# Kv heads in pairs between the row maxima and the output rows of a gated cross-attention block

## The reference

```python
# x and ctx (8, 256, 512) fp32; H = 32 heads of D = 16, HK = 8 kv heads, G = 4 heads to one, T = 256
q = heads(concat([ctx, layernorm(x)]) @ Wq)          # (B, 32, 256, 16)
k, v = heads(layernorm(x) @ Wk), heads(layernorm(x) @ Wv)
ssm_k, ssm_v = heads(ctx @ Wsk), heads(ctx @ Wsv)
scores = einsum('bhqd,bhkd->bhqk', q, concat([ssm_k, k])) / 4 + alibi   # 0 <= q - k < 64, else -inf
o = einsum('bhqk,bhkd->bhqd', softmax(scores), concat([ssm_v, v]))
x = x + tanh(g_xattn) * (o @ Wo)
x = x + tanh(g_ffn) * ffn(layernorm(x))              # router over 128 experts, top 4, a shared part
```

## Time and profile before

| | |
|---|---|
| time before, median of 3 runs | 914.48 us (913.05 to 917.12) |
| time of the profiled execution | 912.41 us |
| its span | 910.5 us |
| TensorE busy (matmul) | 883.1 us, 97% |
| weight loads | 764.3 us, 84% |
| VectorE, ScalarE, GpSimd busy | 568.0, 400.9, 515.8 us |
| mean granted TensorE clock | 0.991 |

### The profile page before, as it was taken

How to read it: one execution, slowest core, us unless ns; L and a number is a source line. 1 busy time by engine, 2 the same in 40 slices (tenths; PEclk the granted TensorE clock), 3 DMA queues, 4 the chain that set the end, 5 groups by cost and what they waited for, 6 DMA issues and landing times.

```text
span 910.5 us, 17708 instructions
## 1 busy us (share of the span) xinstructions
PE 883.1 (97%) x6694; PEld 764.3 (84%) x6694; DVE 568.0 (62%) x1107; ACT 400.9 (44%) x838; POOL 515.8 (57%) x562
## 2 busy tenths in 40 slices
PE   7989999999999999799999999999999999999998
PEld 7878999999999998587888876788888888888886
DVE  6666676767677766672235666565655656556657
ACT  6544545455545554555024243344444444444431
POOL 6561533434343430434188985455887888878731
PEclk9989999999999999999999999999999999999999
DMA  7678476767667565991101144512012120221036
GB/s 239 148 194 211 123 202 152 207 165 204 177 159 221 145 171 139 236 306 65 46 1 47 47 146 146 197 40 77 24 70 70 32 85 23 70 70 27 21 121 248
DMA packets 79358, 115.44 MB, mean 127 GB/s; under 512 B 6561, under 2 KB 49314, under 8 KB 78242
## 3 DMA queue, kind: packets, MB, share of 16 engines
q1 hardware_dynamic: 77000, 113.28, 44.1%
q10 hardware_dynamic: 2274, 1.03, 0.5%
HBM read 75.95 MB, written 36.24 MB: 123 GB/s over the span
## 4 chain that ended last, share of the span: by engine, by line
PE 88%; DMA 3%; SPq 2%; DVE 2%; issue 2%; ACT 2%; POOL 1%; POOLq 0%; DVEq 0%; ACTq 0%
PE ps_scores L2031 19%; PE ps_proj L1701 12%; PE ps_scoresT L2031 10%; PE ps_scores L1690 6%; PE ps_scoresT L1829 6%; PE ps_o L1843 6%; PE ps_scores L1808 6%; PE ps_proj L1690 5%; PE ps_scoresT L1690 5%; PE ps_proj L2031 5%; PE ps_proj L1757 4%; DMA q_stack<-max_rows 1%; SPq L552 1%; DMA w_stage<-in_L_xattn_Wv 1%; PE ps_o_max L1739 1%
## 5 line engine op out<-in xcount | busy, mean ns | idle before, releaser
L1023 ACT ACTIVATE probsT<-ps_scoresT 128x512 f32<-128x512 f32 (+1 forms) x256 | 137.4, 543 | 143.7 <-PE ps_scoresT L1829 143.4
L1347 DVE TENSOR_REDUCE neg_max<-ps_scores 128x2 f32<-128x384 f32 (+1 forms) x256 | 131.9, 517 | 91.9 <-PE ps_scores L1808 88.0
L1233 ACT ACTIVATE part_sums<-ps_scores 128x512 f32<-128x512 f32 x96 | 57.5, 599 | 134.8 <-PE ps_scores L2031 130.4
L1829 PE MATMUL ps_scoresT<-q_stack,k_stack 116*128 116x256 f32 x448 | 104.4, 304 | 10.5 <-ACT probsT L1023 5.8
L1808 PE MATMUL ps_scores<-k_stack,q_stack 114*128 114x192 f32 (+1 forms) x512 | 99.9, 278 | 2.5 <-DVE neg_max L1347 1.2
L1808 PEld LDWEIGHTS ps_scores<-k_stack,q_stack 114*128 114x128 f32 x512 | 82.0, 192 | 13.3 <-DVE neg_max L1347 2.9
L895 POOL TENSOR_TENSOR w_expert_lo<-w_sums,w_expert_hi 128x256 fp32r<-128x256 f32 x64 | 63.8, 1008 | 45.3 <-ACT w_expert_hi L1156 45.3
L907 POOL TENSOR_TENSOR big<-big,basis 128x512 f32<-128x512 f32 x56 | 77.5, 1401 | 15.5 <-DVE basis L1640 15.5
L760 POOL TENSOR_TENSOR oT_lo<-oT_raw,oT_hi 128x256 fp32r<-128x256 f32 x32 | 23.6, 737 | 105.8 <-ACT oT_hi L1034 105.8
L1829 PEld LDWEIGHTS ps_scoresT<-q_stack,k_stack 116*128 116x128 f32 x448 | 71.8, 195 | 12.8 <-issue 6.0
L754 POOL TENSOR_TENSOR o_normal<-o_blocks,inv_sums 128x128 f32<-128x128 f32 x64 | 25.8, 403 | 96.6 <-DVE inv_sums L1367 96.6
(11 more groups left out here) (286 smaller groups left out, 2540.3 us busy)
## 6 DMA issues: line engine op xcount, KB each, us to landing
k_stack<-k_kept SPq DMA_DIRECT2D x64, 192.0 KB, 5.8
q_stack<-q_kept SPq DMA_DIRECT2D x28, 384.0 KB, 5.5
big<-coeff_rows SPq DMA_DIRECT2D x8, 1024.0 KB, 4.8
q_kept<-qT_hi SPq DMA_DIRECT2D x12, 512.0 KB
xn_rows<-in_x SPq DMA_DIRECT2D x8, 512.0 KB, 5.9
k_kept<-kT_hi SPq DMA_DIRECT2D x16, 256.0 KB
x_rows<-in_x SPq DMA_DIRECT2D x8, 512.0 KB, 4.4
x_kept<-x_rows SPq DMA_DIRECT2D x16, 256.0 KB, 5.0
```

Of the source, the lines that this page charges most:

```text
L1023: act.activation(PT[:, g % 2, 2 * j:2 * j + blocks].rearrange("p h f r w -> p (h f r w)"), ST[:, n % 2, 0:blocks].rearrange("p h n -> p (h ...
L1233: act.activation(TP[:, u % 2, j, :], src[:, u % 2, :], ACT.Copy).then_inc(taken, 1)
L1347: dve.tensor_reduce(NM[:, g % 2, 2 * i:2 * i + 2], SA[:, n % 2, :, 0:keys], AX.X, ALU.max, negate=True).then_inc(max_done, 1)
L1829: ins = pe.matmul(ST[:, n % 2, v, :], KS[0:ROWS, g, j + v, 1 - v].rearrange("p w s -> p (w s)"), QS[0:ROWS, g, j + v].rearrange("p f r w - ...
```

## The change

Two neighbouring groups (a **pair**) are taken together from `max_halves` to `o_turn`. `max_halves`, `turn_max`, `max_out` and `stack_max` work on 16 columns of maxima and come once in 8 slots, at 8p + 8, 8p + 9, 8p + 9 and 8p + 10. `times_v` multiplies both groups one behind the other at slot 8p + 26, into the two halves of `ps_o`. `o_turn` turns the whole bank (128x512), `scale_outputs` scales both. The turned maxima move to the free half of the second bank of `ps_scoresT` (a group's last unit needs one half only), so that every odd unit of `scores_turned` waits for `nm_out` as well. `LAG` goes from 14 to 18 and all offsets behind it by 3 or 4 slots; the projections are laid into other slots, since the slots of `times_v` are now twice as long and half as many. `stack_q` reads one group at a time (192 KB), right behind `stack_k` of the same group, both 10 slots ahead of the group's first `scores` (before: keys 14 slots ahead, queries 10 or 14). Each engine's count of instructions: 64 `turn_max`, `max_out`, `stack_max`, `o_turn`, `scale_outputs` become 32; 28 DMAs of `stack_q` become 56.

```diff
-LAG = 14
-NM_TURN, PV, O_TURN, O_BACK, O_HIGH = 6, LAG + 5, LAG + 6, LAG + 8, LAG + 9
+LAG = 18
+PAIR = 2 * NB
+MAX_HALVES, NM_TURN, STACK_MAX = PAIR, PAIR + 1, PAIR + 2
+PV, O_TURN, O_BACK, O_HIGH = LAG + PAIR, LAG + PAIR + 1, LAG + PAIR + 3, LAG + PAIR + 4
 LOAD_ROWS, STATS = -64, (-51, -50)
-CTX_HIGH, CTX_LOW = (-44, -43), (-43, -42)
+CTX_HIGH, CTX_LOW = (-42, -41), (-41, -40)
-Q_PROJ = ((-31, -30, -28), (-27, -26, -24), (-23, -22, -20), (-19, -18, -16))
+Q_PROJ = ((-29, -28, -27), (-26, -25, -24), (-21, -20, -18), (-17, -16, -15))
...
-STACK_K = tuple(4 * g + LAG + 4 - UNITS for g in range(HK))
-STACK_Q = tuple(8 * p + LAG + 8 - UNITS for p in range(PAIRED))
+STACKED = tuple(NB * g + LAG + NB - UNITS for g in range(HK))
...
-def group_due(n, offset):
+def pair_due(n, offset):
...
-    g, rest = divmod(n - offset, NB)
-    return g if rest == 0 and 0 <= g < GROUPS else None
+    p, rest = divmod(n - offset, PAIR)
+    return p if rest == 0 and 0 <= p < GROUPS // 2 else None
+
+
+def max_turns(n):
+
+
+    return max(0, -(-(n - NM_TURN) // PAIR))
...
-ROUTER_AT = {0: 0, 4: 1, 12: 2, 30: 3}
-SHARED_AT = {15: 0, 17: 1, 20: 2, 23: 3, 25: 4, 28: 5}
+ROUTER_AT = {0: 0, 4: 1, 12: 2, 34: 3}
+SHARED_AT = {19: 0, 21: 1, 24: 2, 27: 3, 29: 4, 32: 5}
...
-    PO, PM = POB[:, 0, :], POB[0:4 * NB, 1, 0:P]
+    PM = ST[0:8 * NB, 1, 1, 0:P]
...
-        def stack_q(b, p):
-            gs = slice(2 * p, 2 * p + 2)
+        def stack_q(b, g):
             sp.wait_ge(q_kept, 16 * PARTS * b)
-            sp.wait_ge(st_mm, (b - 1) * UNITS + 2 * NB * (p + 1))
-            sp.dma_start(QS[DATA:FINE, gs].rearrange("p g i f r w -> p g (i f r w)").bitcast(F32),
-                         q_kept_d[b % 2, gs].rearrange("g j d n -> (j d) g n")).then_inc(q_in[p], 16)
+            sp.wait_ge(st_mm, (b - 1) * UNITS + NB * (g + 1))
+            sp.dma_start(QS[DATA:FINE, g].rearrange("p i f r w -> p (i f r w)").bitcast(F32),
+                         q_kept_d[b % 2, g].rearrange("j d n -> (j d) n")).then_inc(q_in[g], 16)
...
-        def turn_max(n):
-            pe.wait_ge(nm_lo, n + 1)
-            if n >= 1:
-                pe.wait_ge(nm_out, n)
-            if n > LEAD - 1:
-                pe.wait_ge(o_turned, n - LEAD + 1)
-            pe.transpose(PM, NMH[:, n % 2].rearrange("p h c -> p (h c)").bitcast(F32), ident[:]).then_inc(nm_t, 1)
+        def turn_max(p):
...
+            unit = PAIR * p + NM_TURN - LAG
+            pe.wait_ge(nm_lo, p + 1)
+            if unit >= 2:
+                pe.wait_ge(exp_done, unit - 1)
+            pe.transpose(PM, NMH[:, p % 2].rearrange("p h c -> p (h c)").bitcast(F32), ident[:]).then_inc(nm_t, 1)
...
+            if n % 2:
+                pe.wait_ge(nm_out, min(max_turns(n + LAG), GROUPS // 2))
...
-        def times_v(n):
-            b, g = divmod(n, HK)
+        def times_v(p):
+            b = p // (HK // 2)
             pe.wait_ge(turn_done, passed("turn_v", b, 0))
-            pe.wait_ge(exp_done, NB * (n + 1))
-            if n >= 1:
-                pe.wait_ge(o_turned, n)
-            pe.wait_ge(nm_out, min(n + LEAD, GROUPS))
-            for j in range(NB):
-                cols_j = min(2 * W, T - j * W)
-                for r in range(G):
-                    ins = pe.matmul(PO[32 * r:32 * r + 2 * D, j * W:j * W + cols_j], VA[:, j, g, :],
...
+            if p >= 1:
+                pe.wait_ge(o_turned, p)
+            for n in (2 * p, 2 * p + 1):
+                pe.wait_ge(exp_done, NB * (n + 1))
+                for j in range(NB):
+                    cols_j = min(2 * W, T - j * W)
+                    for r in range(G):
...
+                ins.then_inc(pv_mm, 1)
```

More of the change, by code:

```diff
@@ L105, in due @@
     return b if rest == 0 and first <= b < B else None
-def group_due(n, offset):
-    g, rest = divmod(n - offset, NB)
-    return g if rest == 0 and 0 <= g < GROUPS else None
+def pair_due(n, offset):
[3 more added lines that the diff above has]
+    return max(0, -(-(n - NM_TURN) // PAIR))
 def split_due(n):
-    found = [p for p in range(GROUPS // 2) if n == O_HIGH + NB * (2 * p + 1) + (NB if p == 0 else 0)]
+    found = [p for p in range(GROUPS // 2) if n == O_HIGH + PAIR * p + (2 if p == 0 else 0)]
     return found[0] if found else None
@@ L133, in x_turn_slot @@
 def x_turn_slot(b, t):
-    return (69, 72)[t] if b < B - 1 else (58, 59)[t]
+    return (73, 77)[t] if b < B - 1 else (62, 63)[t]
 def batch_at(n, slot, first=0):
@@ L301, in build @@
     k_kept, q_kept, pad_kept = sem("k_kept"), sem("q_kept"), sem("pad_kept")
-    stack_in, max_in = ([sem(f"{n}_in{g}") for g in range(HK)] for n in ("stack", "max"))
-    q_in = [sem(f"q_in{p}") for p in range(PAIRED)]
+    stack_in, q_in = ([sem(f"{n}_in{g}") for g in range(HK)] for n in ("stack", "q"))
+    max_in = [sem(f"max_in{p}") for p in range(HK // 2)]
     s_mm, max_done, nm_hi, nm_lo, nm_t, nm_out = (
@@ L599, in _ @@
             for g in range(HK):
-                b = due(n, STACK_K[g], 1)
+                b = due(n, STACKED[g], 1)
                 if b is not None:
                     stack_k(b, g)
-            for p in range(PAIRED):
-                b = due(n, STACK_Q[p], 1)
-                if b is not None:
-                    stack_q(b, p)
+                    stack_q(b, g)
             b = due(n, LOAD_ROWS, 2)
@@ L813, in _ @@
                 x1_normalise(b, 0)
-            m = group_due(n, O_TURN)
-            if m is not None:
-                scale_outputs(m)
+            p = pair_due(n, O_TURN)
+            if p is not None:
+                scale_outputs(p)
             b = batch_at(n, lambda b: x1_roots_slot(b) + (1 if b < B - 1 else 0))
@@ L1111, in _ @@
                 exponentials(n - LAG)
-            m = group_due(n, NM_TURN)
-            if m is not None:
-                max_out(m)
-            m = group_due(n, NM_TURN + 1)
-            if m is not None:
-                stack_max(m)
+            p = pair_due(n, NM_TURN)
+            if p is not None:
+                max_out(p)
+            p = pair_due(n, STACK_MAX)
+            if p is not None:
+                stack_max(p)
             if n == SPLIT_WO:
@@ L1435, in _ @@
         for n in range(SLOTS):
-            m = group_due(n, NM_TURN - 2)
-            if m is not None:
-                max_halves(m)
+            p = pair_due(n, MAX_HALVES)
+            if p is not None:
+                max_halves(p)
             if n < END:
                 maxima(n)
-            m = group_due(n, O_TURN)
-            if m is not None:
-                o_turn(m)
-            m = group_due(n, O_BACK)
-            if m is not None and m % 2:
-                o_back_turn(m // 2)
+            p = pair_due(n, O_TURN)
+            if p is not None:
+                o_turn(p)
+            p = pair_due(n, O_BACK)
+            if p is not None:
+                o_back_turn(p)
             for t in range(TB):
@@ L1801, in scores @@
                 if b >= 1:
-                    pe.wait_ge(q_in[g // 2], 16 * b)
+                    pe.wait_ge(q_in[g], 16 * b)
             if n >= 2:
@@ L1887, in gate_up @@
                 pe.wait_ge(exp_done, END)
+                pe.wait_ge(nm_out, GROUPS // 2)
             if q == FIRST_TILES + 1:
@@ L1918, in _ @@
                 scores(n)
+            p = pair_due(n, PV)
+            if p is not None:
+                times_v(p)
+            p = pair_due(n, NM_TURN)
+            if p is not None:
+                turn_max(p)
             if LAG <= n < END + LAG:
                 scores_turned(n - LAG)
-            m = group_due(n, NM_TURN)
-            if m is not None:
-                turn_max(m)
-            m = group_due(n, PV)
-            if m is not None:
-                times_v(m)
             for t in range(TB):
@@ L1968, in turn_logits @@
                 pe.wait_ge(turn_done, len(TURNS))
-                pe.wait_ge(o_turned, GROUPS)
-                pe.wait_ge(nm_out, GROUPS)
+                pe.wait_ge(o_turned, GROUPS // 2)
             for j in range(4):
```

83 lines of the change are left out of this document (41 added, 42 removed).

## The result

The paired kernel takes 923.54 us in the median (918.34 to 924.71), the kernel before, on the same chip, 914.6 us (913.05 to 917.12): a ratio of 1.0086, with a 95% interval of 1.0048 to 1.0124. It is slower by about 0.9%, where 908.6 was forecast with a range that ended at 917. The profiled execution took 918.34 us, a span of 916.2, at a mean granted clock of 0.987; the others had a clock of 0.980 to 0.983 and spans of 921 to 922.5.

A forecast was written before the change was run, and what follows sets the result against it. TensorE's instruction order and cost were taken as the bound, with DMA engines saturated in the last batch. -14.6 + 6.8 + 1.4 + 0 + 0.5 = -5.9 us gave 906.5 profiled, 908.6 median; range 901.5 to 917.

The forecast's parts named there:

- Savings on TensorE, 0.40 us a pair and 0.12 a turn: TensorE, 28 pairs: fewer layout changes in times_v save 11.2 us and half the turn_max 3.4, together 14.6 us.
- the 2.1 us a batch: Sign to look for in the new profile: a middle batch shorter by 4 x 0.52 = 2.1 us.
- The same goes for the copies, the maxima's halves and the scaling: Work beside o_turn, on an engine with a quarter of its time free: the change there was priced at nothing.
- The last batch, -4 to +5: Maxima's DMA gets 8 slots instead of 7, keys' loads lose 4 of 14; taken to cancel: nothing, from -4 to +5.
- Rival 4: The last batch gets a second long stall, for keys, with the clock behind it: +5 us, 914; chance 0.08.
- The start, 6.8 us given back: Before batch 1's first scores: 4.9 us less work against a fixed gate, 4.5 lost, plus 2.3 for half clock.
- the size of a DMA is hardly the price: Reloads at the start: keys' loads (192 KB) took 5.8 us and queries' (384 KB) 5.5, so size hardly counts.
- The gate in batches 2 to 7: Queries' write and reload before a batch's first scores: no wait, 0.8 us to spare; in batch 7 1.4 us.
- Rival 3: The queries' reload gate closes in every batch: slower by over 0.5%, chance 0.12; milder, 911 to 918, chance 0.17.
- The tail, 0.5 us: Behind the last scores, 18 units of scores_turned instead of 14, mostly covered by TensorE's own work: 0.5 us added.
- Rival 2: Layout changes do not cost the 0.40 us; savings shrink to 3.4 us, median 919.8; chance 0.06.
- rival 1: The gate at the start costs little; 4 to 6 of the 6.8 us stay saved, about 903; chance 0.20.

The follow-up runs named there:

- experiment 3: The paired kernel with CTX_HIGH and CTX_LOW (GpSimd's subtractions) two slots later: 916.37 us, ratio 1.0007 to the kernel before.
- experiment 6: The paired kernel with a pair's two groups of times_v set apart, one ahead of scores_turned and one behind: 931.05 us, ratio 1.0166.
- experiment 1: The paired kernel with ScalarE's splits of the router's and first shared weights moved from slots 18 to 30 to 25 to 32 of the last batch: 911.64 us.
- experiment 4: The kernel before with only the turns of x at slots 73 and 77 and the xT_kept writes at slot 80: 924.85 us, ratio 1.0092.
- the mended kernel: The paired kernel with late splits, CTX_HIGH and CTX_LOW two slots later, and GpSimd's second x1_normalise behind scale_outputs: 906.81 us.
- experiments 9 and 12: The mended kernel with batch 1's first two query groups stacked straight from SBUF, 907.85 us; then also with the q_kept writes behind the first group's stack, 906.18 us.
- Experiment 7: The paired kernel with late splits, CTX_HIGH and CTX_LOW two slots later, and GpSimd's second x1_normalise behind scale_outputs: 906.81 us, ratio 0.9911 to the kernel before.

## Why the prediction was wrong

- **Savings on TensorE, 0.40 us a pair and 0.12 a turn:** right in the main. Of the 2.1 us a batch experiment 3 laid 1.86 bare, and experiment 6 priced a pair's change of layout at 0.33. In the loads of the paired kernel the two late places come once for two groups:

```profile
173.53 0.31 PEld L1810 LDWEIGHTS ps_scores<-k_stack,q_stack 114*128 114x128 f32 x2
173.94 1.58 PEld L1849 LDWEIGHTS ps_o<-probsT,v_ones 128*32 128x32 f32 x64
...
175.62 0.30 PEld L1835 LDWEIGHTS ps_scoresT<-q_stack,k_stack 116*128 116x128 f32 x2
```

  Read as in the earlier trace rows, 173.94 is 0.18 late and 175.62 about as much. What became of the last 0.24 us of the 2.1 is open.
- **"The same goes for the copies, the maxima's halves and the scaling": nothing.** This step failed. The halves' cover was that the turn stood two slots behind them; now it stands one slot behind. They were priced at their usual length, without asking who runs beside them in the new slot. They cost 1.11 us (47.67 less 46.56; TensorE's matmuls stand for 0.87 of it, its weight loads for 1.04) in five batches, 5.6 us by that sum and 7.2 by the medians of experiment 3.
- **The last batch, -4 to +5, "I take one for the other":** this step failed most. The moved `KEEP_X` is in the kernel and was left out of the sum; its DMAs, an engine that waits for them and the exponentials behind it cost 11.9 us between the medians (experiment 1), 9 in the kernel before (experiment 4). Rival 4 had the shape, a second long stall with the clock behind it, but for keys, at +5 and with 0.08.
- **The start, 6.8 us given back:** too much for the traced execution, roughly right in kind. The gate came 2.36 us earlier:

```profile
76.35 0.41 PE L1810 MATMUL ps_scores<-k_stack,q_stack 114*128 114x128 f32 x2 [0.57 <-issue]
```

  With 4.9 us of work less ahead of it, some 2.5 us were given back, and no second stretch at half clock followed (1.00 from 75 to 85). The queries were reread at 73.24, not 74.07, and the idleness lay earlier, where TensorE was held by the halves and by ScalarE (2.47 us at 54.20, 3.73 at 65.74). In the mended kernel the forecast 5.6 us of idleness is there, as 6.80 at 78.73. Whether the size of a DMA is hardly the price stays open: the half reload at the gate landed in 3.0 us and the whole one before in 4.6, but the keys' loads, of the same size as before, fell from 5.8 to 4.4 us in the median as well. That the way through HBM is the price was not borne out: straight from SBUF the gate stayed behind the writes' backlog on the queue (experiments 9 and 12).
- **The gate in batches 2 to 7:** right for 2 to 6, no wait; batch 7 had none either instead of 1.4 us. Rival 3 did not occur.
- **The tail, 0.5 us:** too small. From 400 to 450 us TensorE is idle for 3.7 us against 2.8, 3.5 of it waiting for exponentials, and its clock there is 0.96, where it was 1.00.
- **Rival 2** is out by experiment 6, **rival 1** was true of the gate, and its 4 to 6 us did not show in the time, since two other waits took more.

Experiment 7, with these two waits mended and a third edit, stands at 906.8 us, 0.9% under the kernel before, near the 908.6 forecast. That nearness is partly luck: the start gave back less than forecast in one trace and more in another, and the last batch keeps waits that the sum had at nothing.

## What to carry to other kernels

In a written order, every number of a table is an edit: for each moved DMA, look for the in-order engine that waits for it and what is queued behind, even if it is issued in one batch and waited for in the next. A short instruction that is moved has to be priced beside its new neighbours on the other engines, not at its own median. When a restructuring gains its forecast per step and loses the whole, undo the moved slots one by one before giving up the structure.
